# Two cross-attention layers: scores from pairs of fp32r numbers in two halves of the TensorE array, maxima along rows, heads written out

## What is computed

```
attn = einsum('bhtd,bhsd->bhts', qh, kh) * scale      # 16 heads, 1024 queries, 6404 keys, 8 channels
attn = softmax(attn, axis=-1)
out  = einsum('bhts,bhsd->bhtd', attn, vh)
x = x + tanh(g_xattn[0]) * L0_xattn(layernorm(x), ctx, ctx)
x = x + tanh(g_ffn[0])   * L0_ffn(layernorm(x))       # 8 experts, best 2, gelu
x = x + tanh(g_xattn[1]) * L1_xattn(ctx, ctx, layernorm(x), mask)
x = x + tanh(g_ffn[1])   * L1_ffn(layernorm(x))       # 8 experts, best 2, silu
```

## Time and profile before

| | |
|---|---|
| median of three runs | 3071.01 us (3069.4 to 3073.41) |
| span of the profiled execution | 3066.5 us |
| PE busy in it | 2796.9 us (91%) |
| DVE busy | 2299.4 us (75%) |
| ACT busy | 1853.3 us (60%) |
| POOL busy | 63.1 us (2%) |
| mean granted TensorE clock | 0.939 of full speed |
| chain of work that ended last | PE 82%, issue 5%, DVE 5%, ACT 4%, DMA 3% |

### The profile page before, as it was taken

The page is one execution under the profiler, slowest core; times in us unless marked ns, Lnnn a source line. Parts: engine busy times, 40 slices in busy tenths (PEclk is TensorE's granted clock), DMA queues, the critical chain, the costliest instruction groups (busy, mean ns, idle before and its releaser), DMA issues.

```text
span 3066.5 us, 65440 instructions
## 1 busy us (share of the span) xinstructions
PE 2796.9 (91%) x21032; PEld 1021.1 (33%) x21032; DVE 2299.4 (75%) x2385; ACT 1853.3 (60%) x3513; POOL 63.1 (2%) x150
## 2 busy tenths in 40 slices
PE   2699999999999999996948999999999999999989
PEld 1233333333333333343402333333333333333334
DVE  5788888888888888765458777887777777778524
ACT  2456766766767776663302666666666666666752
POOL 2000000000000000000000000000000000000000
PEclk7789999999999999997956999999999999999989
DMA  6300000000000000013010000000000000000010
GB/s 206 114 1 14 14 14 14 14 14 14 14 14 14 14 14 14 1 59 103 0 53 1 16 14 13 8 9 13 14 14 14 14 14 14 14 14 0 1 56 7
DMA packets 36009, 74.68 MB, mean 24 GB/s; under 512 B 3460, under 2 KB 25240, under 8 KB 33320
## 3 DMA queue, kind: packets, MB, share of 16 engines
q1 hardware_dynamic: 34440, 72.90, 6.7%
q10 hardware_dynamic: 1440, 0.40, 0.1%
HBM read 61.29 MB, written 12.00 MB: 24 GB/s over the span
## 4 chain that ended last, share of the span: by engine, by line
PE 82%; issue 5%; DVE 5%; ACT 4%; DMA 3%; SPq 0%; ACTq 0%; DVEq 0%
PE ps L968 47%; PE ps L1021 26%; PE ps L1137 3%; ACT probs L505 3%; PE ps L1145 3%; DVE m_run L675 1%; DMA k_ring<-k_parts 1%; PE ps L981 1%; DMA q_parts<-probs 1%; PE ps L937 1%; ACT L505 1%; DMA k_parts<-big 0%; PE ps L997 0%; PE ps L989 0%; DVE m_run L621 0%
## 5 line engine op out<-in xcount | busy, mean ns | idle before, releaser
L675 DVE TENSOR_TENSOR m_run<-ps,m_run 128x1024 f32<-128x1024 f32 (+1 forms) x1568 | 1851.5, 1220 | 430.8 <-PE ps L968 422.6
L505 ACT ACTIVATE probs<-ps 128x512 f32<-128x512 f32 (+1 forms) x3264 | 1689.6, 606 | 766.5 <-PE ps L968 716.0
L968 PE MATMUL ps<-q_ring,k_ring 96*128 (+4 forms) x6528 | 1702.3, 392 | 168.7 <-ACT probs L505 84.1
L968 PEld LDWEIGHTS ps<-q_ring,k_ring 96*128 (+4 forms) x6528 | 552.2, 98 | 1338.1 <-issue 448.8
L1021 PE MATMUL ps<-probs,v_head 128*9 128x256 f32 x13056 | 898.5, 383 | 0.5
L1021 PEld LDWEIGHTS ps<-probs,v_head 128*9 128x9 f32 x13056 | 261.8, 89 | 425.4 <-issue 198.2
L680 DVE COPY m_run<-ps 128x1024 f32<-128x1024 f32 x64 | 78.2, 1224 | 50.7 <-PE ps L968 49.6
L505 ACT ACT_TABLE_LOAD x14 | 18.0, 1283 | 142.6 <-PE ps L1088 106.9
L841 DVE TENSOR_TENSOR probs<-probs,k_ring 128x512 f32<-128x512 f32 x64 | 43.7, 691 | 66.1 <-ACT probs L538 57.6
L419 POOL COPY v_head<-v_all 128x108 f32 (+3 forms) x128 | 35.9, 284 | 2603.2 <-PE ps L1021 2467.3
L538 ACT ACTIVATE probs<-ps,b_col 128x512 f32<-128x512 f32 x64 | 43.8, 687 | 67.3 <-PE ps L1137 60.0
(11 more groups left out here) (129 smaller groups left out, 711.4 us busy)
## 6 DMA issues: line engine op xcount, KB each, us to landing
k_ring<-k_parts SPq DMA_DIRECT2D x96, 300.2 KB
k_parts<-big SPq DMA_DIRECT2D x24, 384.0 KB, 3.1
k_ring<-gate_rows SPq DMA_DIRECT2D x16, 512.0 KB, 7.4
probs<-in_mask_t SPq DMA_DIRECT2D x10, 640.0 KB, 4.4
q_ring<-q_parts SPq DMA_DIRECT2D x96, 48.0 KB
big<-in_w SPq DMA_DIRECT2D x1, 2048.0 KB, 10.8
ctx_t<-in_w SPq DMA_DIRECT2D x1, 2048.0 KB, 9.8
ctx_t<-in_ctx_t SPq DMA_DIRECT2D x1, 1666.0 KB, 11.4
```

What stands on the lines that cost most here:

```text
L505: A(probs[0:k, p_slot(t), HALF * half:HALF * half + HALF], ps[0:k, bank, :], ACT.Exp, scale=SCALE).then_inc(sem(f"exp_done{l}"), 1)
L675: V.tensor_tensor(m_run[0:k, t % 2, :], flat(mx(slot)[0:k]), m_run[0:k, t % 2, :], ALU.max).then_inc(sem(f"mx_done{l}"), 1)
L968: return pe.matmul(dst[0:k], key(koff, t, rows), query(qoff, half, rows), start=not masked, stop=True)
```

## The change

Scores are now computed from pairs: a float32 value is the sum of two numbers of the 4-byte type fp32r, a high and a low one, which makes 4 part pairs times 8 channels = 32 rows. One row more holds ones in the keys (33 rows for the maxima), and two more rows stand for the high and low part of the negative maximum (35 rows for the exponentials). Keys stand twice in `k_ring`, in partitions 0 to 34 and 64 to 98; the queries' first half stands in the one, the second half in the other, so two neighbouring matmuls use different halves of the array's rows. The values' matmuls stay fp32, and read `v_all` directly.

For the maxima queries are now the stationary operand and 512 keys move, so a result has queries on its partitions. A unit is one block of 128 queries of each half against a chunk of 512 keys (52 units a head, the chunk of the last four has 260 keys); DVE reduces it along the row to two columns of `m_part`. A head's maximum is then one small reduction and two small instructions (`whole_max`), four transposes on PE into one of the three score banks ("rows") and two copies on ACT (`set_rows`). The running arrays, the join, the eight transposes and `v_head` are gone.

All heads are written out, no hardware loops are left. A step is one key tile: two scores, mostly one maximum unit, the values of the tile two before. Keys are a ring of two heads, loaded in four groups of chunks, 16 DMAs a head and 4 for the queries where there were 3 and 3. The key split needs one instruction each on ACT and DVE. The layer-norm temporaries, `x_t`, `y_t` and the gate arrays moved to other memory; POOL alone restores the ring's rows before layer 1.

```diff
-PARTS = 3
-KR = PARTS * HD
-QKR = PARTS * KR
-MROW = 96
-ROWS_MAX = MROW
-ROWS_EXP = MROW + PARTS
+PARTS = 2
+KR = PARTS * PARTS * HD
+ROWS_MAX = KR + 1
+ROWS_EXP = KR + 3
+HB = 64
+KW = NT * P
+KRING = 2
+QRING = 3
...
-STEP = 2
-NSTEP = -(-NT // STEP)
-PSLOTS = 5
-EXB = 3
+PSLOTS = 6
+EB = 3
+LAG = 2
...
-        k_ring = sb("k_ring", [P, RING * TK], BF16)
-        q_ring = sb("q_ring", [P, RING * TQ], BF16)
+        k_ring = sb("k_ring", [P, KRING * KW], F32R)
+        q_ring = sb("q_ring", [P, QRING * HALF], F32R)
...
+                for n, row in enumerate((KR, HB + KR)):
+                    nc.gpsimd.memset(k_ring[row:row + 32, 0:wide].bitcast(F32), 1.0).then_inc(sem("ring_set"), 1)
...
-            def split(f, parts, rest, w):
-
-                link(V.tensor_tensor(rest[:, 0:w], f[:, 0:w], parts[:, 0, 0:w], ALU.subtract))
-                link(V.tensor_copy(parts[:, 1, 0:w], rest[:, 0:w]))
-                return V.tensor_tensor(parts[:, 2, 0:w], rest[:, 0:w], parts[:, 1, 0:w], ALU.subtract)
+            def low_half(parts, bank, bias, w):
+
+                return V.scalar_tensor_tensor(out=parts[:, 1, 0:w], in0=bank[:, 0:w], scalar=bias,
+                                              in1=parts[:, 0, 0:w].bitcast(F32), op0=ALU.add, op1=ALU.subtract)
...
+            def max_tile(l, n, h, j):
+
+                c, p = j // NPAIR, j % NPAIR
+                dve.wait_ge(sem(f"mx_filled{l}"), n + 1)
+                V.tensor_reduce(m_part[:, h % 2, :, p, c], mx(n % 2)[:, :, 0:chunk_w[c]], AX.X, ALU.max
+                                ).then_inc(sem(f"mx_done{l}"), 1)
...
+                V.tensor_reduce(m_neg[:, :, :], m_part[:, h % 2, :, :, :], AX.X, ALU.max, negate=True
+                                ).then_inc(sem(f"m_whole{l}"), 1)
...
+            def score(l, unit, masked):
...
+                row, koff, qoff = HB * half, h % KRING * KW + P * t, h % QRING * HALF
...
+                pe.matmul(bank, k_ring[row:row + ROWS_EXP, koff:koff + P], q_ring[row:row + ROWS_EXP, qoff:qoff + HALF],
+                          start=not masked, stop=True).then_inc(sem(f"scored{l}"), 1)
...
+                for half in range(2):
+                    row, bank = HB * half, mx(n % 2)[:, half, :]
...
+                    mm = pe.matmul(bank[:, 0:w], q_ring[row:row + ROWS_MAX, qoff:qoff + P], k_ring[row:row + ROWS_MAX, koff:koff + w],
+                                   start=not masked, stop=True)
+                mm.then_inc(sem(f"mx_filled{l}"), 1)
...
-                with pe.Fori(0, LOOP) as h:
-                    head(l, h, pe.snap(h * MXU + FIRST), masked, mx_steps(True))
-                head(l, H - 2, LAST2, masked, mx_steps(False))
-                head(l, H - 1, LAST, masked, [["out"] if s == 1 else [] for s in range(NSTEP)], l == 0)
+                for h in range(H):
+                    for t, (units, scores) in enumerate(zip(max_units(h), score_units(h))):
+                        for unit in scores:
+                            score(l, unit, masked)
+                        for unit in units:
+                            m_unit(l, unit, masked)
+                        if l == 0 and h == H - 1 and t >= 4 + LAG and (t - LAG) % 4 == 0:
+                            next_layer((t - LAG) // 4 - 1)
+                        n = h * NT + t - LAG
+                        if n >= 0:
+                            weigh(l, n // NT, n % NT)
```

More of the change, by code:

```diff
@@ L16 @@
 F32 = mybir.dt.float32
+F32R = mybir.dt.float32r
 BF16 = mybir.dt.bfloat16
@@ L52 @@
 KST = 3
-RING = 3
-STEP = 2
-NSTEP = -(-NT // STEP)
-PSLOTS = 5
-EXB = 3
-V_CHUNKS = [(0, 12), (12, 24), (24, 36), (36, NT)]
-AHEAD = 8
-ENDING = [[("next", 0)], ["turn", ("next", 1)], [("next", 2), ("next", 3)], ["rows", ("next", 4)],
-          [("next", 5)], [("next", 6), ("next", 7)]]
-ENDING_UNITS = sum(ENDING, [])
-AFTER_ROWS = len(ENDING_UNITS) - 1 - ENDING_UNITS.index("rows")
-STEP_OUT = 1
-STEPS_OF_3 = (4, 8, 12, 16)
-MXU = NT + 3
-def mx_steps(ahead):
-    steps, t = [], AHEAD
-    for s in range(NSTEP - len(ENDING)):
-        n = 1 if s == 0 else 3 if s in STEPS_OF_3 else 2
-        steps.append([("max", t + i) for i in range(n)] + ["out"] * (s == STEP_OUT))
-        t += n
-    assert t == NT
-    return steps + [[u for u in step if ahead or isinstance(u, str)] for step in ENDING]
@@ L85 @@
-P_FIVES = NT - 4 * (-NT % 5)
-def p_slot(t):
-    return t % 5 if t < P_FIVES else (t - P_FIVES) % 4
-def p_before(t):
-    return max(u for u in range(-NT, t) if p_slot(u % NT) == p_slot(t))
-assert MXU % 2 == 0 and AHEAD % 2 == 0 and 2 * NT % EXB == 0
-assert P_FIVES % 5 == 0 and (NT - P_FIVES) % 4 == 0 and all(t - p_before(t) >= 4 for t in range(NT))
-BF_ONES = float(np.array([0x3F803F80], np.uint32).view(np.float32)[0])
+PSLOTS = 6
+EB = 3
+LAG = 2
+KCH = -(-TK // HALF)
+NPAIR = HALF // P
+NU = KCH * NPAIR
@@ new lines, with max_units @@
+AHEAD = 8
+OUT_AT = 4
+ROWS_AT = 47
+K_GROUPS = [(0, 3), (3, 6), (6, 9), (9, KCH)]
+def max_units(h):
+    seq = [("max", h + 1, j) for j in range(AHEAD, NU)] if h + 1 < H else []
+    seq += [("max", h + 2, j) for j in range(AHEAD)] if h + 2 < H else []
+    if h:
+        seq.insert(min(OUT_AT, len(seq)), ("out", h - 1, 0))
+    steps = [[] for _ in range(NT)]
+    for i, unit in enumerate(seq):
+        steps[max(i * NT // max(len(seq), NT), OUT_AT if unit[0] == "out" else 0)].append(unit)
+    return steps
@@ new lines, with score_units @@
+FIRST_UNITS = [("max", 0, j) for j in range(NU)] + [("max", 1, j) for j in range(AHEAD)]
+UNITS = FIRST_UNITS + [u for h in range(H) for step in max_units(h) for u in step] + [("out", H - 1, 0)]
+UNIT_AT = {u: n for n, u in enumerate(UNITS)}
+def score_units(h):
+    steps = [[("score", h, 2 * t), ("score", h, 2 * t + 1)] for t in range(NT)]
+    if h + 1 < H:
+        steps[ROWS_AT].append(("rows", h + 1, 0))
+    return steps
+SCORES = [("rows", 0, 0)] + [u for h in range(H) for step in score_units(h) for u in step]
@@ L102 @@
+SCORE_AT = {u: n for n, u in enumerate(SCORES)}
 MCH = 5
@@ new lines, in exp_all @@
+            def exp_all(l):
+                set_rows(l, ("rows", 0, 0))
+                for h in range(H):
+                    for t, step in enumerate(score_units(h)):
+                        for unit in step:
+                            if unit[0] == "rows":
+                                set_rows(l, unit)
+                            else:
+                                exp_unit(l, unit)
+                        if h and t == LAG - 1:
+                            evacuate(l, h - 1)
+                evacuate(l, H - 1)
@@ L572, in _ @@
             exp_all(0)
+            for n in range(KST):
+                act.wait_ge(sem(f"k_stored1_{n}"), 16 * len(range(n, NCH, KST)))
             turned("o0", 0, x_t)
@@ L740, in maxima @@
-                o_norm(l, H - 1, LAST, 0)
-                dve.wait_ge(sem(f"mx_done{l}"), LAST + 1)
+                for n, (kind, h, j) in enumerate(UNITS[:-1]):
+                    if kind == "out":
+                        o_norm(l, n, h)
+                    else:
+                        max_tile(l, n, h, j)
+                        if j == NU - 1:
+                            whole_max(l, h)
                 if l == 0:
```

498 lines of the change are left out of this document (195 added, 303 removed).

## The result

The changed kernel takes 4048.1 us (median; 4043.7 to 4050.7) where the kernel before takes 3071.7 (3069.4 to 3073.4). The ratio is 1.318, 95% interval 1.316 to 1.320. The forecast was 2536 us with a range of 2410 to 2830, so the sign was wrong too. Of the kernels under Experiments each ran once, the last one four times, and always on the same chip as the kernel before, which took 3068 to 3073 us.

The account below looks back on a forecast made before the run. TensorE bound the kernel before; VectorE would bound the changed one, at 62.5 us a head. Savings of 508 us in the layers and 27 at the starts, 535 from 3071, gave 2536 us, range 2410 to 2830.

Parts of the forecast that it names:

- the granted clock: TensorE in the heads: assumed to stay at 1.00 and 0.95, as in earlier stretches with value matmuls between.
- The clock rival: TensorE in the heads at 1.2 GHz: a step near 2 us, time near 3600 us; chance 0.03.
- TensorE's step: One key tile in the heads: two overlapping score pairs at 0.2156 us plus one tile's values, 1.09 us.
- Weight loads: Rival, score pairs: fp32 weight loads show, step 1.38 us, time 2800 us (1.30 and about 2680 by the skill); chance 0.12.
- VectorE: Maxima in the heads: reductions 1.15 us each, 59.1 us a head; VectorE sets the pace, 62.5 with the tie's loss.
- Loop ends: Layer 1, between heads: TensorE's 5.63 us waits at 14 loop ends vanish, some 79 us.
- Starts: Start of each layer: 18 us saved in layer 0, leaving 6 of the mask stall, and 9 in layer 1.

Follow-up runs that it names:

- the last one: Changed kernel with 64 rows in every score matmul and the mask's transfers issued ahead of head 1's and head 2's loads: 2660.8 us, ratio 0.867 to the kernel before.
- a run without load price: Changed kernel with 64 rows in every score matmul and the scores' operands read as bf16 (less precise output): 2518.0 us.

## Why the prediction was wrong, point by point

**The step that failed is the granted clock.** Every TensorE term was taken from rows at 1.00, and that the heads would still run there was argued in one sentence, "with value matmuls between, the stretches at 300 and 1700 have 1.00 and 0.95". That sentence read the wrong cause out of the earlier trace rows. In those stretches the scores used 96 to 99 rows, and the change cuts them to 33 and 35; the value products alone don't hold the clock, as every run at 0.50 shows. With rows of zeros and nothing else the kernel runs at 1.00 and takes 2680 us, which lies within the forecast range. The clock rival named the lower clock and its sign in the profile, "a granted clock near 0.5 within the heads", but looked for its cause in missing value matmuls and not in the rows, and got a chance of 0.03. Its size, 3600 us, was too small: I had rounded the step down to "near 2 us", where 1.09 doubled is 2.18 and 2.13 was measured. The miss adds up: from the first exponential pair to the last transposes the layers take 1735 us (188.1 to 1922.9) and 1732 us (2190.5 to 3922.4), together 3467 where I had 1996. So 1471 of the 1512 us lie in the heads, and 41 in what is around them.

**TensorE's step, in cycles: right.** One record per fp32r matmul (L916 x3264, two for each of 1632 tiles), 0.43 us at 1.2 GHz, halves overlapping (0.43 us a pair saved against both in one half). Forecast 1.09 at full clock, 1.07 by halving the measured step. But the closeness is in part luck, since the measured step holds a load price that I hadn't counted: without it, in bf16, half the step is 0.97.

**Weight loads: dismissed, and there.** At full clock the step is 1.22, not 1.09, with 0.34 us pair to pair against 0.25 with bf16; at 0.50 it was 0.59 against 0.41. I had priced this rival at 1.38 from the earlier trace rows, 0.29 us over my step, and given it 0.12. The mechanism was right, and of the size 0.09 is left (1.22 against bf16's 1.13). The Trainium skill's rule on fast weight loads ("TensorE: Matmul & The Clock Gate", sections Weight-path perf modes, and LDWEIGHTS for the 107 ns), by which I had 1.30, is also above the 1.22. The 2680 us that I gave beside it is what the run with 64 rows takes, by coincidence: its layers take 2101 us, less than that step would give, and its starts more than I had forecast.

**VectorE: right in size.** Reductions take 1.145 us where 1.15 was forecast, though only in the bf16 run with 64 rows does VectorE catch up with TensorE; in the changed kernel it idles. The head of a run without load price is 60.5 us where I had 62.5 (58.4 if nothing is lost). That run, with clock and loads both as I assumed them, takes 2518 us against my 2536. That is closer than its terms: the layers take 1947 us (182.4 to 1168.0 and 1434.4 to 2395.5) where I had 1996, 49 less, and the rest 31 more, so two errors cancel in part.

**Loop ends: right.** Nothing of the 5.63 us of the earlier trace rows is left, 800.00 of 800 us busy in layer 1. At 0.50 the gain is only swallowed.

**Starts: wrong.** I left 6 of the 15.54 us stall; it became 31.65. The mask's transfers stood behind other loads, as I had said, but these are 24 DMAs (head 1's queries and keys, head 2's queries), of which the 16 of the keys take 26.29 us to issue, 1.64 us each, where I had reckoned with 0.78. In layer 1 TensorE waits 35.3 us for the first queries where it waited 33.17, so nothing of the 9 us came either.
